# Attention scores from two float32r parts in four 32-row strips of TensorE

## What is computed

```python
x = x + _L1_ffn_ref(_layernorm(x, axis=-1), ...)      # "moe": biased q, k, v, then experts
x = x + _L1_attn_b_ref(_layernorm(x, axis=-1), ...)   # "rms": q and k through rms_norm
x = x + _L1_ffn_ref(_layernorm(x, axis=-1), ...)      # "moe"
...
q = (src @ Wq + bq).reshape(B, T, N_HEAD, HEAD_DIM)   # 16 heads of 8 channels
scores = jnp.einsum('bqhd,bkhd->bhqk', q, k) * scale
probs = jax.nn.softmax(scores, axis=-1)
attn = jnp.einsum('bhqk,bkhd->bqhd', probs, v).reshape(B, T, D_MODEL)
```

## Time and profile before

| | |
|---|---|
| time, median of 3 runs | 4721.38 us (4718.21 to 4732.62) |
| span of the profiled execution, first to last instruction | 4609.9 us |
| `stream` in it | 2012 us to the end, units from 2074 to 4466 us |
| busy in the span: PE, DVE, ACT, POOL | 3765.8, 3223.7, 2810.4, 1146.2 us |
| median minus span | 111.5 us |

### The profile page before, as it was taken

How to read it: one execution, slowest core, us unless ns; L and a number is a source line. 1 busy time by engine, 2 the same in 40 slices (tenths; PEclk the granted TensorE clock), 3 DMA queues, 4 the chain that set the end, 5 groups by cost and what they waited for, 6 DMA issues and landing times.

```text
span 4609.9 us, 92060 instructions
## 1 busy us (share of the span) xinstructions
PE 3765.8 (82%) x36864; PEld 1564.1 (34%) x36864; DVE 3223.7 (70%) x4668; ACT 2810.4 (61%) x5452; POOL 1146.2 (25%) x1376
## 2 busy tenths in 40 slices
PE   4888976677677687838999898989999999989872
PEld 1334443234243355522223232323222222333232
DVE  4777734664654577519987877777979999888921
ACT  2676832431422455415877778787988988768761
POOL 3212001011001023231133443433121122352413
PEclk7999988888888778757999999999999999999996
DMA  2222101110100000011132313131111111313213
GB/s 83 62 54 62 20 17 24 23 24 1 23 2 0 8 1 1 1 55 20 51 85 52 98 46 95 42 95 42 47 46 20 48 50 23 106 47 95 62 44 97
DMA packets 141118, 204.34 MB, mean 44 GB/s; under 512 B 51906, under 2 KB 88770, under 8 KB 140436
## 3 DMA queue, kind: packets, MB, share of 16 engines
q1 hardware_dynamic: 123924, 137.97, 12.2%
q0 software_dynamic: 16768, 60.49, 4.3%
HBM read 123.34 MB, written 64.68 MB: 41 GB/s over the span
## 4 chain that ended last, share of the span: by engine, by line
PE 55%; DVE 21%; issue 6%; ACT 6%; POOL 4%; DMA 4%; SPq 3%; POOLq 0%; DVEq 0%; ACTq 0%
PE ps L1170 12%; DVE stream_max_pieces L1370 8%; PE ps L1143 8%; PE ps L1155 5%; PE ps L598 3%; PE ps L1948 3%; PE ps L557 2%; PE ps L1256 2%; PE ps L240 2%; PE ps L1264 2%; PE ps L2696 2%; DVE mamba_conv_sum L2991 1%; SPq L874 1%; PE ps L578 1%; ACT stream_probs L1282 1%
## 5 line engine op out<-in xcount | busy, mean ns | idle before, releaser
L1370 DVE TENSOR_REDUCE stream_max_pieces<-ps 128x2 f32<-128x1024 f32 x1536 | 1793.1, 1214 | 312.6 <-PE ps L1155 301.0
L1282 ACT ACTIVATE stream_probs<-ps 128x512 f32<-128x512 f32 x3072 | 1653.7, 600 | 333.3 <-PE ps L1143 310.7
L1170 PE MATMUL ps<-stream_probs,stream_v 128*16 128x256 f32 x12288 | 982.3, 392 | 33.4 <-issue 32.2
L1155 PE MATMUL ps<-stream_k_stack,stream_q_stack 48*128 48x512 bf16 x3072 | 656.6, 394 | 109.9 <-DVE stream_max_pieces L1370 77.6
L1143 PE MATMUL ps<-stream_q_stack,stream_k_stack 51*128 51x512 bf16 x3072 | 676.1, 394 | 27.0 <-ACT stream_probs L1282 10.3
L737 DVE TENSOR_REDUCE alibi_max_pieces<-ps 128x2 f32<-128x1024 f32 (+3 forms) x384 | 355.4, 952 | 142.8 <-PE ps L582 133.3
L678 ACT ACTIVATE alibi_probs<-ps 128x512 f32<-128x512 f32 (+3 forms) x768 | 333.8, 492 | 176.8 <-PE ps L563 142.5
L1170 PEld LDWEIGHTS ps<-stream_probs,stream_v 128*16 128x16 f32 x12288 | 203.5, 94 | 663.1 <-issue 362.6
L1143 PEld LDWEIGHTS ps<-stream_q_stack,stream_k_stack 51*128 51x128 bf16 x3072 | 181.6, 93 | 669.2 <-ACT stream_probs L1282 500.3
L362 POOL CAST stream_negmax_parts<-stream_negmax_t 128x32 bf16<-128x32 f32 x96 | 23.0, 240 | 1134.4 <-DVE stream_negmax_t L1359 1088.7
L1155 PEld LDWEIGHTS ps<-stream_k_stack,stream_q_stack 48*128 48x128 bf16 x3072 | 157.9, 95 | 160.8 <-DVE stream_max_pieces L1370 121.8
(11 more groups left out here) (448 smaller groups left out, 5410.0 us busy)
## 6 DMA issues: line engine op xcount, KB each, us to landing
stream_q_terms_dram<-stream_q_parts SPq DMA_DIRECT2D x72, 256.0 KB
stream_k_terms_dram<-stream_k_parts SPq DMA_DIRECT2D x72, 256.0 KB
stream_q_stack<-stream_q_terms_dram SPq DMA_DIRECT2D x96, 192.0 KB, 4.5
stream_k_stack<-stream_k_terms_dram SPq DMA_DIRECT2D x96, 192.0 KB, 4.5
delta_v_shifted<-delta_v_padded SPq DMA_DIRECT2D x64, 158.0 KB, 3.5
alibi_q_terms_dram<-alibi_q_parts SPq DMA_DIRECT2D x24, 256.0 KB
alibi_k_terms_dram<-alibi_k_parts SPq DMA_DIRECT2D x24, 256.0 KB
alibi_q_stack<-alibi_q_terms_dram SPq DMA_DIRECT2D x32, 192.0 KB
```

The lines of the kernel that those rows point to most:

```text
L1155: ins = e.matmul(c.ps[:, mbank(key) + r, :], qs[R, buf, pair, qt * P:(qt + 1) * P], ks[R, buf, pair, kh * 512:kh * 512 + 512], start=True, ...
L1170: ins = e.matmul(c.ps[32 * j:32 * j + 16, 7, Q], v[:, b % 2, kt, GH * g + j, :], pr[:, (u + j // 2) % RP, j % 2, Q], start=(n == 0 and k = ...
L1282: e.activation(pr[:, u % RP, r, :], c.ps[:, ebank(key), :], ACT.Exp, scale=SCALE).then_inc(s_ed, 1)
L1370: e.tensor_reduce(mx[:, j % 2, kh, 4 * pair + qt % 4, :], c.ps[:, mbank(key):mbank(key) + 2, :], AXX, ALU.max).then_inc(s_md, 1)
```

## The change

q and k are split into two parts of type float32r, high (a copy, rounded to the type) and low (what is left, computed in place in `full`). Three products (high-high, high-low, low-high) make a score: 24 contraction rows, and two more (26) with the negated maximum in two parts. A head's rows then fit into a strip of 32 partitions; the four heads of a group lie on four strips (partition 64 * pair + 32 * r), and the pairs no longer share partitions. The maximum runs 41 units ahead rather than 40; since `pair` alternates, the maximum's two matmuls of a unit are then on the two strips that the exponent's two don't use. Row counts in bytes stay equal: 24 rows of 4 KB for each of 4 heads, where 48 rows of 2 x 2 KB stood for each of 2. The ones come from a memset of the k stack on VectorE instead of six DMAs.

```diff
+HALF_Q = (0, 0, 1)
+HALF_K = (0, 1, 0)
+HTERMS, HROWS, MROWS = 3, 3 * HD, 2
+def halves(e, chain, src, high, low):
+    chain(e.tensor_copy(high, src))
+    chain.sync()
+    return chain(e.tensor_tensor(low, src, high, ALU.subtract))
...
-        return 5 if self.kind(n) == "rms" else 4
+        return 3 if self.kind(n) == "rms" else 2
...
-    plan = Stream(CHAIN, 40)
+    plan = Stream(CHAIN, 41)
-    KM = TERMS * HD
-    KE = KM + 3
+    KM = HROWS
+    KE = KM + MROWS
...
-    parts = [sb(n + "_parts", [P, 3, L], BF16) for n in "qk"]
+    high = [sb(n + "_high", [P, L], F32R) for n in "qk"]
-    qs = sb("q_stack", [P, RQ, 2, L], BF16)
-    ks = sb("k_stack", [P, RQ, 2, L], BF16)
+    qs = sb("q_stack", [P, RQ, L], F32R)
+    ks = sb("k_stack", [P, RQ, L], F32R)
...
-                R = slice(64 * r, 64 * r + KE)
+                R = slice(64 * pair + 32 * r, 64 * pair + 32 * r + KE)
...
-                R = slice(64 * r, 64 * r + KM)
+                R = slice(64 * pair + 32 * r, 64 * pair + 32 * r + KM)
...
+        e.memset(ks[:, :, :].bitcast(F32), 1.0).then_inc(s_set, 1)
...
-        for buf in range(RQ):
-            for r in range(2):
-                e.dma_start(ks[64 * r + KM:64 * r + KE, buf, :, :], c.ins["ones3"]).then_inc(s_ones, 16)
-        e.wait_ge(s_ones, 96)
...
-            for r in range(2):
+            for j in range(GH):
                 for dst, src in ((qs, qd), (ks, kd)):
-                    e.dma_start(dst[64 * r:64 * r + KM, buf, :, :], src[s, r].rearrange("i (d a) t -> (i d) a t", a=2)).then_inc(s_ld[buf], 16)
+                    e.dma_start(dst[32 * j:32 * j + KM, buf, :].bitcast(F32), src[s, j].rearrange("i d t -> (i d) t")).then_inc(s_ld[buf], 16)
```

More of the change, by code:

```diff
@@ L6 @@
 F32 = mybir.dt.float32
+F32R = mybir.dt.float32r
 BF16 = mybir.dt.bfloat16
@@ L1139, in scores @@
             for r in range(2):
-                R = slice(64 * r, 64 * r + KE)
+                R = slice(64 * pair + 32 * r, 64 * pair + 32 * r + KE)
                 key = ("unit", u, r)
                 take_e(key)
-                e.matmul(c.ps[:, ebank(key), :], ks[R, buf, pair, kt * P:(kt + 1) * P], qs[R, buf, pair, h * 512:h * 512 + 512], start=True, stop=True).then_inc(s_ef, 1)
+                e.matmul(c.ps[:, ebank(key), :], ks[R, buf, kt * P:(kt + 1) * P], qs[R, buf, h * 512:h * 512 + 512], start=True, stop=True).then_inc(s_ef, 1)
         def max_scores(u):
@@ L1153, in max_scores @@
             for r in range(2):
-                R = slice(64 * r, 64 * r + KM)
-                ins = e.matmul(c.ps[:, mbank(key) + r, :], qs[R, buf, pair, qt * P:(qt + 1) * P], ks[R, buf, pair, kh * 512:kh * 512 + 512], start=True, stop=True)
+                R = slice(64 * pair + 32 * r, 64 * pair + 32 * r + KM)
+                ins = e.matmul(c.ps[:, mbank(key) + r, :], qs[R, buf, qt * P:(qt + 1) * P], ks[R, buf, kh * 512:kh * 512 + 512], start=True, stop=True)
             ins.then_inc(s_mf, 1)
@@ L1307, in scalar @@
             elif kind in ("q", "k"):
-                wait(e, s_ch[i], plan.split_base(n))
+                wait(e, s_pw[i], 16 * HTERMS * n)
                 if rms:
@@ L1357, in turn @@
             e.wait_ge(s_nm, j + 1)
-            wait(e, s_mch, 4 * (j - 1))
+            wait(e, s_mch, 2 * (j - 1))
             e.transpose(nmt[:, j % 2, :], nm[:, j % 2, :]).then_inc(s_nmt, 1)
@@ L1503, in max_split @@
                 e.wait_ge(s_mw, 64 * (j - 1))
-            cm.at(4 * j)
-            split(e, cm, nmt[:, j % 2, :], [nmp[:, j % 2, i, :] for i in range(3)], nmr[:, :], c)
+            cm.at(2 * j)
+            halves(e, cm, nmt[:, j % 2, :], nmp[:, j % 2, 0, :], nmp[:, j % 2, 1, :])
         def split_step(n, i, k):
             src, chain, rms = full[i][:, :], ch[i], plan.kind(n) == "rms"
-            part = [parts[i][:, r, :] for r in range(3)]
             if k == 0:
@@ L1516, in split_step @@
                     return
-            k -= plan.splits(n) - 4
             chain.sync()
-            if k == 0:
-                wait(e, s_pw[i], 96 * n)
-                chain(e.tensor_copy(part[0], src))
-            elif k == 1:
-                if i:
-                    e.wait_ge(s_ch[0], plan.split_base(n + 1))
-                elif n:
-                    e.wait_ge(s_ch[1], plan.split_base(n))
-                chain(e.tensor_tensor(rest[:, :], src, part[0], ALU.subtract))
-            elif k == 2:
-                chain(e.tensor_copy(part[1], rest[:, :]))
+            if k == plan.splits(n) - 2:
+                wait(e, s_pw[i], 16 * HTERMS * n)
+                chain(e.tensor_copy(high[i][:, :], src))
             else:
-                chain(e.tensor_tensor(part[2], rest[:, :], part[1], ALU.subtract))
+                chain(e.tensor_tensor(src, src, high[i][:, :], ALU.subtract))
         def scale(n, k):
@@ L1626, in max_rows @@
                     k = 8 * r + 4 * pair
[L1627 removed]
+                    at = 64 * pair + 32 * r
+                    e.dma_start(qs[at + KM:at + KE, buf, half * 512:half * 512 + 512].bitcast(F32).rearrange("r (t q) -> r t q", t=4),
                                 md[par, k:k + 4].rearrange("t r i u -> r t (i u)")).then_inc(s_mr[par], 16)
@@ L1653, in sync @@
             elif kind == "store":
-                for i, (dst, order) in enumerate(((qd, PAIR_Q), (kd, PAIR_K))):
+                for i, (dst, order) in enumerate(((qd, HALF_Q), (kd, HALF_K))):
                     e.wait_ge(s_ch[i], plan.split_base(n + 1))
                     for k, p in enumerate(order):
-                        e.dma_start(dst[n * NG:(n + 1) * NG, :, k].rearrange("g r m t -> (g r) m t"), parts[i][:, p, :]).then_inc(s_pw[i], 16)
+                        e.dma_start(dst[n * NG:(n + 1) * NG, :, k].rearrange("g r m t -> (g r) m t"), (full[i][:, :] if p else high[i][:, :].bitcast(F32))).then_inc(s_pw[i], 16)
     core.add("tensor", tensor)
```

27 lines of the change are left out of this document (12 added, 15 removed).

## The result

The changed kernel takes 4876.44 us (median of 4 executions, 4854.08 to 4916.95) beside 4720.61 us before: **1.033 times as long, interval 1.027 to 1.039**. The forecast was 4658 us.

A forecast was written before the change was run, and what follows sets the result against it. PE alone was taken to bind units with a side job; PE, VectorE and ScalarE finish light units together. Terms -36 - 10 - 18 - 1 + 2 = -63 us gave 4658 us, forecast's own range 4615 to 4695, overall 4600 to 4715.

The forecast's parts named there:

- The group: Exponent's and maximum's matmuls in a unit: four strips stream together, 0.53 to 0.41 us, saving 36 us over side-job units.
- The Trainium skill's four tiles at 3.07 times one: Counter-estimate for the four strips' streams: only 0.065 us saved a unit, some 18 us less gain, 4676 us.
- 277 job units: Stream units with a side job, counted from the plan, where PE alone binds and 0.13 us each is saved.
- The wait for sorted tokens: PE's 24.2 us of waits at L1248: a chain ending 4 to 6 us earlier saves 18 us, bounds 0 and 24.
- the start: Start of the stage: first split 6.3 us shorter, against memset, extra loads and one more maximum; together -1 us.
- The stores: Six stores for 12 on SP's queue in the token chain: 0 to 5.4 us saved, the middle only as cover.
- The lower clock: Units at half clock, up to 96 in 188 us, each 0.31 us shorter: 10 us saved, with the clock staying 0.96.
- the clock falls in light units: Rival: PE, idler in units without a side job, loses the full clock, +0.51 us each; 4811 us at 300; chance 0.07.
- end of the stage: Last 41 units, with no maximum beside them: the longer load is not covered by a saved stream; +2 us, at most +4.
- the forecast's upper end: Upper end of the side-job saving: float32r loading as fast as bf16, 0.22 us a unit, 61 us.
- the distance of 111.5 us: Gap between the trace's span of 4609.9 us and the median time, assumed to stay the same after the change.
- The rival of slow streams: Rival: float32r streams at two or four cycles a column, or strips not together; 4774 or 5420 us; chances 0.06 and 0.02.

The follow-up runs named there:

- e13: The kernel before, unchanged, run again beside the others on one chip: 4619.0 us, ratio 1.001.
- e16: The changed kernel with filled strips (exponent's product over 32 rows for 26, maximum's over 30 for 24), on the same chip: 4600.66 us, ratio 0.997.
- e14: The changed kernel, not altered further, run again beside the kernel before on one chip: 4800.62 us, ratio 1.042.
- Stretch 6 of the second patterns: Constant matmuls put ahead of the changed kernel's stage: its float32r unit, 48 times, after 24 full bfloat16 matmuls raised the clock; it kept 1.00.
- stretch 3 of the first patterns: Constant matmuls put ahead of the changed kernel's stage: two bfloat16 halves of 51 rows, twice, plus the values' matmuls (unit of before); the clock rose.
- stretch 7: Constant matmuls put ahead of the changed kernel's stage: four float32r strips together without the values' matmuls; the clock rose, a group cost 0.47 us back to back.
- stretch 1: Constant matmuls put ahead of the changed kernel's stage: four float32r strips together plus the values' matmuls (its own unit), 24 units; the clock stayed at 1.2 GHz.

## Why the prediction was wrong

**The group: right in kind beside a job, wrong in light units.** Four strips stream together, the load is 181 ns as the float32 row had it, and behind a side job the group is 0.44 us (0.41 forecast). Units with an expert job went from 2.18 to 2.08 us, 0.10 for 0.13. The Trainium skill's four tiles at 3.07 times one ("TensorE: Matmul & The Clock Gate", Part 3, "Measured speedup vs the span model"), by which the estimate had 0.065, was off by as much to the other side. In light units the group got longer, 0.64 to 0.67 for 0.57, since the load behind a bank wait is not hidden. And the plan's count of 277 job units left out the transposes of the outputs inside `unit` (L1189): the trace has 358 units with a job, 77 of them with these transposes alone, and those went from 1.71 to 1.85 us.

**The wait for sorted tokens and the start: right in kind, more than forecast.** PE's wait at that line in e13 and in e16:

```profile
PE ps L1248 <- DMA stream_slots<-stream_slots_dram: 56.3, 8, 35.7
```

```profile
PE ps L1261 <- DMA stream_slots<-stream_slots_dram: 35.8, 2, 35.6
```

Without the last batch's 35.7, for which nothing hides, 20.6 us became 0.2 (18 forecast). That the shorter chain did it is not shown: the kernel before with a lead of 41, at the higher level, has 37.4 us with the same 35.7 in it. TensorE's idle time ahead of the first maximum fell from 29.87 to 19.66 us, by 10; forecast were 6.3 less 1.6. The stores, which the forecast took only as cover, have most of the rest: from the split's last operation to the first load it is 13 us in e13 and 9 in e14.

**The lower clock: the step that failed.** The sum took the clock for given: 0.96 stays, and the units that fall under it get shorter ("I take 10 us"). It asked only whether PE, idler in light units at the full clock, would *fall*, compared busy shares (0.86 of 1.13 us), found them on the safe side and gave that rival 0.07. The busy share was the wrong measure. Stretch 6 of the second patterns shows that the unit keeps a full clock, as the forecast argued; and the first one shows that it doesn't regain it while 100% busy. The kernel before had the same falls (26 for 29), but its units, with streams of 102 and 96 rows one after the other and short loads, bring the clock back, as stretch 3 of the first patterns shows. So the term "units at the lower clock", -10 us for 188 us that were to stay, became 1000 us of lower clock. The rival "the clock falls in light units" (0.07) had the price about right: 0.51 us a unit forecast, 1.71 - 1.13 = 0.58 measured, 4811 us at 300 units; 385 light units came. Its mechanism, that light units lose the clock, was not what happened.

**Sum.** The three traces of one chip can be laid side by side unit by unit, since all have the same 1536 units in the same order. Time against e13, in us; "full" is a unit wholly at the full clock in both traces, give or take 0.3 us:

| part | forecast | changed (e14) | filled (e16) |
|---|---|---|---|
| ahead of the stage (no difference in the program) | 0 | 0 | -7 |
| start of the stage, to the first values | -1 | -8 | -5 |
| 21 units with token transposes | -18 | -27 | -32 |
| other job units, full | -36 | -16 | -17 |
| units with output transposes alone, full | not counted | +7 | +9 |
| light units, full | 0 | +13 | +12 |
| units at the full clock in e13 and not here (283 and 53) | 0 | +169 | +26 |
| units at the lower clock in e13 already | -10 | -8 | -4 |
| end of the stage | +2 | 0 | 0 |
| span (the parts are rounded) | -63 | +130 | -17 |

So one line, the clock, turns a small gain into the loss. The traced execution of e14 is the quickest of its four; the medians are 182 us apart, and the slower three have a lower clock (0.821 to 0.833 over the span, for 0.846). With the clock nearly back (e16) the gain is 17 us by the traces, 7 of them from ahead of the stage, and not 63: light units and output transposes take back most of what the other jobs gain. The bfloat16 strips, whose load is 92 ns, show the forecast's upper end: expert-job units of 1.97 us, 0.21 less, light units of 1.13 as before, and 91 us in all.

**The level.** Keeping the distance of 111.5 us was a guess that cancelled here, since neither kernel has it, but it hid that the trace read was of an execution 100 us faster than those timed.

**The rival of slow streams** never came up: in stretch 7 at the full clock a group of four float32r matmuls of 512 columns starts every 0.23 us, where bfloat16 streams of 512 columns came 0.22 us apart.

## What to carry to other kernels

Ask two questions of TensorE's clock: does a pattern keep it, and does it regain it after a wait? Packing matmuls into strips shortens busy time, but fewer rows stream in it; where loads then lie open, as here, full strips, even of zeros, were worth 156 us more than 26 rows. The version that beats both kernels here is two bfloat16 parts in four strips (0.981 on two chips), if 16 bits of q and k are enough; with float32r the filled strips are level with before.

## What the runs showed that was not expected

A TensorE at 100% busy can stay at 1.2 GHz (38.7 us in stretch 1, 60 us at 99.8% in the kernel). Rows of zeros count for the clock: 26 to 32 rows turned 0.81 into 0.92 over the stage. A float32r load of 128 columns takes 181 ns, like float32, though the stream goes at bfloat16's pace. And one kernel has levels of 4617 and 4720 us on different chips, and its versions shift with it, by 76 to 120 us.
